# Centring the tokens of a wavelet stage with two single-pass products in place of one float32 product

## The reference, cut to what matters

```python
def _ln_c(v, eps=1e-06):
    m = jnp.mean(v, axis=1, keepdims=True)
    s = jnp.var(v, axis=1, keepdims=True)
    return (v - m) / jnp.sqrt(s + eps)
...
    x = x + _L0_conv_ref(_ln_c(x), L0_conv_s_ll, L0_conv_s_lh, L0_conv_s_hl, L0_conv_s_hh, L0_conv_w1, L0_conv_b1, L0_conv_w2, L0_conv_b2)
    t = _to_tokens(x)
    t = t + _L0_ffn_ref(_ln_t(t), L0_ffn_gate_w, L0_ffn_gate_b, L0_ffn_weight1, L0_ffn_weight2)
```

## Time and profile before

| what | value |
|---|---|
| median of 3 runs | 2119.15 us (2116.65 to 2120.28) |
| the profiled execution: its own time | 2120.05 us |
| the profiled execution: its span | 2118.2 us |
| PE busy in the span | 2006.2 us, 95% |
| DVE, ACT, POOL busy | 1189.5, 1005.5, 511.4 us |
| wavelet stage: first PE product to last token square root | about 16.7 to 334.5 us |

### The profile page before, as it was taken

The page is one execution under the profiler, slowest core; times in us unless marked ns, Lnnn a source line. Parts: engine busy times, 40 slices in busy tenths (PEclk is TensorE's granted clock), DMA queues, the critical chain, the costliest instruction groups (busy, mean ns, idle before and its releaser), DMA issues. The chain is left out here.

```text
span 2118.2 us, 41606 instructions
## 1 busy us (share of the span) xinstructions
PE 2006.2 (95%) x14926; PEld 1535.6 (72%) x14926; DVE 1189.5 (56%) x2548; ACT 1005.5 (47%) x2815; POOL 511.4 (24%) x622
## 2 busy tenths in 40 slices
PE   6999993599999989999999999999999799999998
PEld 3555551367777779999999999999999544444443
DVE  4777777756666652222222222232222399999998
ACT  4666664343434423333344444444444555555552
POOL 4555553222222210000000000000000455555552
PEclk9999996599999999999999999999999799999999
DMA  3955551132222200000000000000000256666653
GB/s 110 243 166 164 165 156 54 56 100 85 96 95 86 100 31 12 0 0 0 0 4 0 0 0 0 12 9 0 0 0 0 79 151 158 159 155 163 159 147 90
DMA packets 192676, 159.10 MB, mean 75 GB/s; under 512 B 25848, under 2 KB 159000, under 8 KB 192536
## 3 DMA queue, kind: packets, MB, share of 16 engines
q1 hardware_dynamic: 190840, 156.89, 26.4%
q0 software_dynamic: 512, 0.53, 0.1%
q10 hardware_dynamic: 1184, 0.00, 0.0%
HBM read 56.70 MB, written 67.11 MB: 58 GB/s over the span
## 5 line engine op out<-in xcount | busy, mean ns | idle before, releaser
L1208 PE MATMUL s_ps<-g_ring,g_T 128*128 128x128 f32 x7620 | 855.7, 274 | 8.5 <-DVE g_ring L1255 8.5
L1208 PEld LDWEIGHTS s_ps<-g_ring,g_T 128*128 128x128 f32 x7620 | 854.6, 191 | 9.2 <-DVE g_ring L1255 9.1
L1244 DVE SCALAR_TENSOR_TENSOR g_ring<-s_ps,s_xs 128x128 f32<-128x128 f32 x508 | 148.4, 292 | 418.6 <-PE s_ps L1208 418.6
L1307 ACT ACTIVATE g_X<-g_ring 128x256 f32<-128x256 f32 x254 | 172.4, 679 | 295.9 <-DVE g_ring L1244 295.9
L1687 DVE TENSOR_TENSOR tm_Z<-tm_pg,tm_nd 128x1024 f32<-128x1024 f32 x256 | 301.7, 1210 | 7.5 <-PE tm_pg L1527 6.3
L1541 PE MATMUL tm_po<-tm_Z,g_wexp 128*64 128x512 f32 x1024 | 249.3, 608 | 0.0
L1291 ACT ACTIVATE g_X<-g_ring 64x256 f32 x256 | 106.8, 417 | 205.6 <-DVE g_ring L1244 203.3
L1244 DVE SCALAR_TENSOR_TENSOR g_ring<-s_ps,g_X 128x128 f32<-128x128 f32 x254 | 74.0, 291 | 211.1 <-PE s_ps L1208 211.1
L1623 POOL TENSOR_TENSOR g_X<-g_x,g_X 128x512 f32<-128x512 f32 x64 | 82.9, 1297 | 349.4 <-POOLq L1184 286.0
L1302 ACT ACTIVATE s_xs<-g_X 128x256 f32<-128x256 f32 x254 | 161.3, 636 | 0.6 <-PEq L1184 0.6
L1541 PEld LDWEIGHTS tm_po<-tm_Z,g_wexp 128*64 128x64 f32 x1024 | 62.5, 137 | 109.8 <-issue 107.9
(11 more groups left out here) (273 smaller groups left out, 2879.5 us busy)
## 6 DMA issues: line engine op xcount, KB each, us to landing
tm_nd<-g_X SPq DMA_DIRECT2D x256, 128.0 KB, 2.4
g_X<-in_x SPq DMA_DIRECT2D x128, 128.0 KB, 2.9
x1s<-g_X SPq DMA_DIRECT2D x64, 256.0 KB, 2.1
x1tok<-g_X SPq DMA_DIRECT2D x64, 256.0 KB, 2.5
g_x<-x2s SPq DMA_DIRECT2D x64, 256.0 KB, 2.9
y<-tm_yo SPq DMA_DIRECT2D x128, 128.0 KB, 2.5
g_X<-x1s SPq DMA_DIRECT2D x32, 256.0 KB, 2.8
x2s<-g_X SPq DMA_DIRECT2D x32, 256.0 KB, 2.0
```

Of the source, the lines that this page charges most:

```text
L1208: last = pe.matmul(out, g.T[i][:, d * P:d * P + P], g.ring[(u - 1) % RING][:, images(c), d:d + 64], start=(d == 0), stop=(d == ND - 1))
L1244: dve.scalar_tensor_tensor(g.ring[n % RING][:, images(c), inner], conv, 0.0, x[:, images(c)], ALU.max, ALU.add).then_inc(y_ready[c], 1)
L1307: act.activation(line(*place(n)), g.ring[n % RING][:, :, inner], ACT.Copy).then_inc(stored, 1)
```

## The change

Token centring gets the form that the first centring already has. DVE rounds x1 to fp32r (`high_of_token`, a CAST), POOL subtracts (`low_of_token`), and PE multiplies both parts with `Cmr` in two single-pass products. The products for chunk c move from step c+3, ahead of the transposes, to step c+4, directly behind the centring of the chunk of that step and ahead of the variance products. The token squares, the gate's logits and the token variances move one step later with them, and the scaled logits and MAX8 too. Two tiles with two buffers each, `th` and `tl`, are added. SP's load of a chunk also waits for the remainder of the chunk that held the buffer before.

```diff
             def _(pe):
...
-                    wait(pe, s["tln"], (c - 2) // 2)
+                    wait(pe, s["tln"], (c - 3) // 2)
...
                 def token_centre(c):
+                    wait(pe, s["tparts"], c + 1)
+                    wait(pe, s["tsquared"], c)
+                    pe.matmul(tc[:], Cmr[:], th[c % 2], start=True, stop=False)
+                    pe.matmul(tc[:], Cmr[:], tl[c % 2], start=False, stop=True).then_inc(s["tcentred"], 1)
+
+                def turn(c):
                     wait(pe, s["x1"], c + 1)
-                    wait(pe, s["tsquared"], c)
-                    pe.matmul(tc[:], g.Cm[:], buf(c), start=True, stop=True).then_inc(s["tcentred"], 1)
-
-                def turn(c):
                     wait(pe, s["tcopied"], c)
...
                 for c in steps:
                     if now(c):
                         centre(c)
+                    if now(c - 4):
+                        token_centre(c - 4)
                     if now(c - 1):
                         variance(c - 1)
                     if now(c - 2):
                         low(c - 2)
-                    if now(c - 4) and c % 2 == 1:
-                        gate_logits((c - 4) // 2)
-                        token_variance((c - 4) // 2, c - 2)
+                    if now(c - 5) and c % 2 == 0:
+                        gate_logits((c - 5) // 2)
+                        token_variance((c - 5) // 2, c - 2)
                     if now(c - 3):
-                        token_centre(c - 3)
                         turn(c - 3)
...
             def _(pool):
...
+                def low_of_token(c):
+                    wait(pool, s["thigh"], c + 1)
+                    wait(pool, s["tcentred"], c - 1)
+                    pool.tensor_tensor(tl[c % 2], buf(c), th[c % 2].bitcast(F32), ALU.subtract
+                                       ).then_inc(s["tparts"], 1)
...
                     if now(c):
                         low_of_square(c)
+                    if now(c - 3):
+                        low_of_token(c - 3)
                     if now(c + 2):
                         low_of_x(c + 2)
...
+                def high_of_token(c):
+                    dve.wait_ge(s["x1"], c + 1)
+                    wait(dve, s["tcentred"], c - 1)
+                    dve.tensor_copy(th[c % 2], buf(c)).then_inc(s["thigh"], 1)
```

More of the change, by code:

```diff
@@ L337, in wavelet_mixer @@
             "centred", "squared", "var", "lnv", "rstd", "normed", "low", "low_s", "rec", "x1",
-            "high", "parts", "xhigh", "xparts", "tcentred", "tsquared", "tturned", "tcopied", "logits", "tvar",
+            "high", "parts", "xhigh", "xparts", "thigh", "tparts", "tcentred", "tsquared", "tturned", "tcopied", "logits", "tvar",
             "tln")}
@@ L345, in wavelet_mixer @@
         xr, sq, rr, nn, lowS, tsq, ts, trs = g.xr, g.sq, g.rr, g.nn, g.lowS, g.tsq, g.ts, g.trs
+        th, tl = ([m.sb(f"{n}{i}", [P, N], F32R)[:] for i in range(2)] for n in ("th", "tl"))
         tok_dst = g.x1tok.rearrange("b j w x -> b w j x")
@@ L363, in load @@
                     wait(sp, s["logits"], (c - XBUFS) // 2 * 2 + 2)
+                    wait(sp, s["tparts"], c - XBUFS + 1)
                     for t in range(2):
@@ L523, in _ @@
                         rstd(c - 1)
[L524 to L527, removed]
+                    if now(c - 5) and c % 2 == 0:
+                        token_rstd((c - 5) // 2)
+                    if now(c - 4):
+                        token_square(c - 4)
             @block.gpsimd
@@ L594, in _ @@
                     high_of_x(c)
-                for c in range(CHUNKS + LAG + 1):
+                for c in range(CHUNKS + LAG + 2):
                     if now(c - 3):
@@ L601, in _ @@
                         high_of_x(c + 2)
[L602 to L605, removed]
+                    if now(c - 3):
+                        high_of_token(c - 3)
+                    if now(c - 6) and c % 2 == 1:
+                        scale_logits((c - 6) // 2)
+                    if c >= 8 and c % 2 == 0:
+                        block_top((c - 8) // 2)
                     if now(c - 1):
```

## The result

The changed kernel takes 2158.86 us (median of 4 runs, 2156.42 to 2160.65) against 2119.72 us beside it (4 runs, 2116.65 to 2121.89). The ratio is 1.0185, with a 95% interval from 1.0167 to 1.0203. It is slower by 39 us. The forecast was 2141. The range reached up to 2160 only because it took in the first rival, which had 2158, and it is this rival that came true, not the working behind the forecast.

A forecast was written before the change was run, and what follows sets the result against it. PE was taken as the bound; waits would lengthen a pair of steps from 9.52 to 10.22 us, +21.0 over 30 pairs, plus 1.3 at the drain: 2142.4 from 2120.05, less 0.90, forecast 2141 us, range 2124 to 2160.

The forecast's parts named there:

- the first rival: The third CAST waits for POOL's subtraction of the square; a pair of steps takes 10.73 us, total 2158 us; chance 0.25.
- PE's 31 us become waiting time: On PE, two single-pass token products save 0.49 us in each of 64 steps, 31 us, all turning into waiting.
- The third CAST, where DVE keeps its turn: DVE runs the third CAST directly behind the second, so POOL's subtraction of the square is held 0.34 us longer.
- X' to X'': From the plain step's token products to the next gate step's, through DVE and POOL: 4.75 us.
- the operation of 0.28 us that took 1.37: Trace evidence: a DVE operation, median 0.28 us, took 1.37 when started 0.07 us into a POOL subtraction.
- rows 8: Trace rows where two DVE copies finished after both POOL memsets, taken to show that the engine at work goes on.
- the 0.90 that the forecast took off: The profiled execution's 2120.05 us was taken as 0.90 above the median of the runs shown.
- X to X' through ACT: From the gate step's token products to the plain step's, through the token variances and ACT's three operations: 5.47 us.
- The 0.10 for a first product behind a wait: On PE, a first product behind a wait was taken to last about 0.10 us longer.
- A gain of 0.49 us per step on PE: Two single-pass token products take 0.47 us where the float32 token product takes 0.96.
- The faster rival: POOL's token remainder is there whenever PE asks; a pair of steps takes 8.87 us, total 2102 us; chance 0.10.
- the one without change: Waits just fill what PE saves; a pair of steps takes 9.45 to 9.55 us, total 2120 us; chance 0.07.

The follow-up runs named there:

- The run in which POOL asks later: Changed kernel with POOL's subtraction of the square also waiting for the second CAST; 2146.01 us, ratio 1.0126.
- The run with the unused CAST behind the two others: Kernel before, plus a CAST of x1 on DVE whose result nobody uses, directly behind the CASTs of the square and input; 2147.97 us, ratio 1.0139.
- both moves: Changed kernel with the CAST of x1 ahead of the CAST of the square on DVE and the token products behind the low mixing on PE; 2112.70 us, ratio 0.9974.
- with ACT: Changed kernel with the token products behind the low mixing on PE and ACT instead of DVE rounding x1; 2110.19 us, ratio 0.9964.

## Why the prediction was right in its sign and its range, and wrong in its forecast

*PE's 31 us become waiting time*: right. The token products went from 0.96 to 0.47 us between starts, while the stage grew by 39 us. PE's busy time, whose ends are modelled, fell only from 309 to 306 us and tells little of either.

*The third CAST, where DVE keeps its turn*: this is the step that failed. I took from two copies beside two memsets that the engine at work goes on with its next instruction, and put 0.34 us on POOL. POOL had issued its subtraction 0.17 us before the third CAST, and DVE paid 1.08 us. The run in which POOL asks later shows this directly. That part of the pair, X' to X'', was 4.75 in the forecast and 5.34 in the run (169.04 to 174.38), and it went over the normalisation and the centring, where the forecast had it go over POOL. The rule from the Trainium skill (SBUF — State Buffer, "Who interferes with whom"), which I had beside the first rival, was the better evidence, and so was the operation of 0.28 us that took 1.37: it told of two single instructions of the two engines, as here, where rows 8 told of memsets, and in a stage start.

Rows 8 didn't carry over to POOL's subtractions either. In the run with the unused CAST behind the two others, POOL starts its second subtraction at 205.48, 0.04 before the first ends, while the CAST has stood there since 204.31. The CAST ends at 205.81 all the same, 0.29 behind the first subtraction, and the second one takes 1.46 us instead of 1.27. So POOL doesn't keep its turn past a waiting CAST with a second subtraction, as it did past a waiting copy with a second memset. Why the memset went ahead wasn't tested and stays open.

*The first rival*: right in place, order and nearly in size. Its terms against the rows of the timeline: the CAST ends 2.19 behind the CAST of the square (measured 2.18), the normalisation 3.41 (3.37), the next centring 0.15 later (0.15). From the token products of the gate step to those of the plain step 5.47 (163.59 to 169.04, 5.45), then to the CAST of the square 1.23 (1.27), then to the token products 4.03 (170.31 to 174.38, 4.07). The pair 10.73 (10.78). The total of 2158 is worked out on the profiled execution, 2120.05 + 36.3 + 1.3, without the 0.90 that the forecast took off; on the forecast's footing it is 2157, against a median of 2158.86. That it came within 1 us of the median is in part luck.

*X to X' through ACT*: right in its way, and in its size because two terms cancel. PE starts L448 at 169.04, 0.15 behind the end of the token square (168.89), where 0.05 was put down: that term came from a wait for POOL, and such a wait took 0.05 in a later run too (169.39 to 169.44). The 0.10 for a first product behind a wait isn't there at X, where the token products follow the centring without a wait (0.47). So 0.47 + 2.96 + 0.04 + 1.83 + 0.15 makes the measured 5.45, against 5.47. Without ACT's three operations the step would, as an estimate, be only 0.20 shorter, since the way over DVE is almost as long.

*X' to X'' through POOL*: in the changed kernel DVE is later still, so nobody waits for this way. Where POOL asks a little later it comes out as put down: from the CAST of the square to the token products 0.51 + 0.34 + 2.62 + 0.05 = 3.52 in the forecast and 3.53 in that run (165.91 to 169.44), there as 0.91 + 2.57 + 0.05. Its pair is 10.36 and not 10.22: the whole part is 4.80 there (from L448 at 164.64) for 4.75, and the part through ACT 5.57 (to L448 at 175.01) for 5.47; there the 0.10 is in its place, and the 0.05 is 0.15.

*A gain of 0.49 us per step on PE*: right for products directly behind others (163.59 to 164.06, 0.47), wrong where they follow a wait of their own; there the gain is 0.30 us, and the groups beside them get longer. This decided how little the best versions gain.

*The faster rival and the one without change*: the condition of the faster rival came true, but not its price. The token remainder is in time in both steps (POOL ends it at 172.57 + 1.26 = 173.83, for one, and PE starts L448 at 174.38), though only because the normalisation, and with it PE, comes later still. The rival without change needed the token square in time, and it isn't: it holds PE by 0.20 in each plain step.

*What would show it*: of my signs, PE's wait for ACT before L448 and its lower busy share (306 of 353 us, 87%) came true, but both hold for the first rival too. The ones that belong to the forecast alone didn't: PE doesn't wait for `wm_tl` at L448, the pair is 10.78 and not 10.2, and the square's subtraction is at 1.39 and not 1.7. The sign of the first rival, a third CAST of 1.4 us or more, is what the profile shows.

## What to carry to other kernels

When an operation is added to DVE, look not only at its own busy time and DVE's gaps but at what POOL is doing when it is issued. Here the same CAST costs 0 or 29 us depending on its place among three. When an instruction of DVE takes far longer than an equal one, as 1.50 us against 0.42 here, look for a wait within it, though the profile counts it as busy. And a cheaper product on the bound engine is worth only what the longest way around through the other engines leaves: here the best step seen is 4.60 us on average, down from 4.76, and not 4.27.

## What the runs showed that I had not expected

A stage can have two collisions of this kind that hide one another. With the third CAST gone from DVE (on ACT), the CAST of the square waits 0.74 us in one step of two for the subtraction of the input, and with the CAST of x1 moved ahead, that one waits itself: its mean of 0.84 is 0.43 in one kind of step and about 1.25 in the other. In these traces a CAST that has waited ends 0.28 or 0.29 us behind the subtraction that held it, as at 166.96 and 166.68, or 155.02 and 154.73.

The versions with both moves and with ACT end the stage about 9 us earlier than the kernel before (last MAX8 at 326.76 and 326.27 instead of 335.29), but their medians are lower by only 5 to 8 us, and their executions spread over 5 to 6 us. The stages behind, which are the same instructions, differ by some us from execution to execution. The profiled executions of these two versions were the fastest of their 8 and 7 runs (2107.60 and 2106.99 us). In the profiled executions the three last scans took, from their first product to their last, 860.5 us with both moves, 863.7 before and 866.5 with the change. The cause is open.
